# Memory stage of a macaron block: VectorE's second retrieve product in front of the residual store and the inverse deviation

## What is computed

```
x = x + 0.5 * ffn(layernorm(x))
x = x + attn(layernorm(x))
x = x + 0.5 * ffn(layernorm(x))

attn(x): keys   = (x @ Wk.T + bk) as 64 quaternions, each divided by its norm
         values = (x @ Wv.T + bv) as 64 quaternions
         memory = cumsum over positions of quat_mul(values, keys)
         r = quat_mul(memory, quat_conj(keys)) / sqrt(position)
         return x + (layernorm(r) * ln_g + ln_b) @ Wo.T + bo
ffn(x):  xr, xk = mixes of x and x of the position before
         return sigmoid(xr @ W_r) * (square(relu(xk @ W_k)) @ W_v)
```

## Time and profile before

| | |
|---|---|
| median of 3 runs | 636.75 us (635.14 to 639.82) |
| the profiled execution | 636.66 us |
| its span | 634.9 us |
| mean granted TensorE clock | 0.997 |
| first feed-forward, memory stage, second feed-forward | about 0 to 184, 184 to 460, 460 to 635 us |

### The profile page before, as it was taken

One profiled execution on the slowest core, in us unless ns is written; L12 is line 12 of the kernel. 1 busy time (PEld: TensorE's weight loads), 2 busy tenths in 40 slices (PEclk: granted clock), 3 DMA queues, 4 the chain that ended last, 5 costly groups with the idle time before them and its releaser, 6 DMA issues.

```text
span 634.9 us, 12143 instructions
## 1 busy us (share of the span) xinstructions
PE 607.8 (96%) x3284; PEld 513.9 (81%) x3285; DVE 561.6 (88%) x1160; ACT 466.9 (74%) x858; POOL 530.6 (84%) x616
## 2 busy tenths in 40 slices
PE   6999999999987999999999999998889899999997
PEld 4888898989866787778778777877668789898896
DVE  6999999998878999999999999999988778787773
ACT  5767677776567888888888888887467767777662
POOL 1788989887748999999999999998938898888863
PEclk9999999999998999999999999999999999999999
DMA  8740000000000000000000000000001111010111
GB/s 236 246 149 2 0 0 0 0 0 1 2 1 1 0 3 0 0 0 0 0 0 0 0 0 0 0 0 1 0 2 35 34 66 66 33 66 33 67 67 66
DMA packets 19272, 18.65 MB, mean 29 GB/s; under 512 B 1328, under 2 KB 19248, under 8 KB 19248
## 3 DMA queue, kind: packets, MB, share of 16 engines
q1 hardware_dynamic: 19248, 18.36, 9.1%
HBM read 9.97 MB, written 8.39 MB: 29 GB/s over the span
## 4 chain that ended last, share of the span: by engine, by line
PE 46%; POOL 27%; issue 19%; ACT 4%; DVE 3%; POOLq 1%; ACTq 0%; DVEq 0%
PE bank L1295 24%; PE bank L1343 16%; POOL rhalf L289 7%; POOL ret L296 6%; POOL kact L278 5%; POOL bhalf L271 4%; PE bank L1316 4%; POOL bhalf L269 1%; ACT xn L825 1%; POOL xr_lo L1152 1%; POOL rhalf L287 1%; PE bank L1286 1%; PE bank L1479 1%; PE bank L1362 1%; POOL xk_lo L303 0%
## 5 line engine op out<-in xcount | busy, mean ns | idle before, releaser
L1343 PE MATMUL bank<-wffn,kact 128*128 128x256 f32 x512 | 117.0, 382 | 3.3 <-DVE kact L427 3.3
L1423 PE MATMUL bank<-wkv,m_xnT 128*128 128x256 f32 x480 | 117.9, 389 | 2.1 <-ACT m_xnT L953 2.1
L1423 PEld LDWEIGHTS bank<-wkv,m_xnT 128*128 128x128 f32 x480 | 89.9, 192 | 24.2 <-ACT m_xnT L953 8.5
L1343 PEld LDWEIGHTS bank<-wffn,kact 128*128 128x128 f32 x512 | 95.0, 190 | 16.0 <-DVE kact L427 3.7
L303 POOL TENSOR_TENSOR xk_lo<-xk,xk_hi 128x1024 fp32r<-128x1024 f32 x30 | 71.0, 2368 | 40.4 <-ACT xk_hi L841 40.3
L1159 POOL TENSOR_TENSOR res<-res,gating_buffers 128x1024 f32 (+1 forms) x31 | 74.6, 2406 | 12.8 <-DVE gating_buffers L434 12.5
L645 DVE TENSOR_TENSOR xn<-bank,khat 128x1024 f32<-128x1024 f32 x64 | 77.7, 1216 | 2.1
L645 DVE TENSOR_TENSOR gating_buffers<-bank,khat 128x1024 f32<-128x1024 f32 x64 | 77.4, 1211 | 0.0
L1152 POOL TENSOR_TENSOR xr_lo<-xr,xr_hi 128x1024 fp32r<-128x1024 f32 x30 | 71.1, 2370 | 1.5
L1479 PE MATMUL bank<-wo_centred,normedT 128*128 128x256 f32 x256 | 66.3, 388 | 4.9 <-DVE res L682 2.1
L1295 PE MATMUL bank<-wffn_hi,xr_hi 128*128 128x256 f32 x240 | 67.4, 281 | 0.0
(11 more groups left out here) (143 smaller groups left out, 1597.6 us busy)
## 6 DMA issues: line engine op xcount, KB each, us to landing
res<-x SPq DMA_DIRECT2D x15, 512.0 KB, 4.2
out<-res SPq DMA_DIRECT2D x15, 512.0 KB, 2.9
res<-x SPq DMA_DIRECT2D x2, 256.0 KB, 2.9
out<-res SPq DMA_DIRECT2D x2, 256.0 KB, 2.1
wffn<-w_k SPq DMA_DIRECT2D x1, 256.0 KB, 5.0
wffn<-w_r SPq DMA_DIRECT2D x1, 256.0 KB, 5.7
wo<-w_o SPq DMA_DIRECT2D x1, 256.0 KB, 6.0
wffn<-w_v SPq DMA_DIRECT2D x1, 256.0 KB, 6.3
```

The costliest lines, as they stand in the source:

```text
L1343: last = nc.tensor.matmul(dst[:, i, :], x[:, f, i * P:(i + 1) * P], wffn[:, w, f, :], start=f == 0, stop=f == FC - 1)
L1423: last = nc.tensor.matmul(dst[:, i, :], m_xnT[:, f, i * P:(i + 1) * P], wkv[:, f, col:col + D], start=False, stop=f == FC - 1, skip_group_ ...
```

## The change

In VectorE's list of the memory stage, retrieve(j, b, 1) moves up by two places: it is issued right behind key_sum, ahead of the store of s - 3 and of ln_inverse of s - 1. All else, waits and semaphores too, is as before. The last step's own branch is untouched.

```diff
--- before.py
+++ after.py
@@ -718,11 +718,11 @@
                             next_stats(0)
                         if has(b, 2):
                             key_sum(j + 1, b)
+                        retrieve(j, b, 1)
                         if has(b, -3):
                             store_x(*at(j, b, -3))
                         if behind:
                             ln_inverse(*at(j, b, -1))
-                        retrieve(j, b, 1)
                         if has(b, 2):
                             key_inverse(j + 1, b)
```

## The result

The changed kernel takes 662.02 us in the median (661.12 to 662.96, 4 runs) against 637.47 before: ratio 1.038, 95% interval 1.036 to 1.040. Forecast were 660.2 us and a range of 656 to 665. The profiled execution has a span of 660.1 us against 634.9, 25.2 more.

A forecast was written before the change was run, and what follows sets the result against it. VectorE was taken to set the memory stage's pace, with the loop through the store just below; 22.6 us for 26 transitions plus 0.9 on the way out gave 23.5 on 636.66, so 660.2 us, range 656 to 665.

The forecast's parts named there:

- The store already is on time by a hair, and the loop through it is the second bound: Memory stage: PE's output waits for VectorE's store L682; that loop lies just below VectorE's own work, slack 0.25 us.
- The two numbers behind it: Loop from store through PE, ScalarE and VectorE back to store: 8.29 us without the product, 9.41 with it.
- What is late next is VectorE, retrieve 0 waits some 0.8 us: VectorE's first product of a memory-stage step would wait some 0.8 us for PE's sum_upto.
- retrieve 1 earlier, cost and gain nothing: VectorE's second product starts 0.67 us earlier for GpSimd's rhalf, which comes to it in its turn; gain 0.
- L615 costs nothing: VectorE's reciprocal, 1.12 us later, feeds ScalarE's ret_normalize, which has 0.8 us idle behind it; cost 0, other end 0.3.
- 22.6 us for 26 transitions: Memory stage, stores of s = 3 to s = 29: 26 steps, each going from 8.54 to 9.41 us.
- The way out, 0.9: At s = 30 PE's output and the store behind it come later; 0.9 us, bounds 0 and 1.0.
- Rival C, the clock falls: PE idling before each output lowers its clock, each step's keys take 3.54 us; 43 us more, 703 us; chance 0.04.
- the step with the added statistics: Near the memory stage's end (s = 28), statistics precede the store; led by VectorE's branch, +0.86 us, like the other steps.
- Rival A: Memory stage: VectorE's occupancy is the bound and PE absorbs the push; no change, 636.7 us; chance 0.07.
- B: PE's slack before the output counts in full, 0.31 us a step, 8 in all; 645 us; chance 0.05.
- D: VectorE's second product held the step; earlier, it removes a GpSimd-related wait, 6 us faster, 630.7 us; chance 0.03.

The follow-up runs named there:

- e1_store_first: Changed kernel with the store put back ahead of retrieve 1, leaving only the move past the inverse deviation; 637.52 us, ratio 0.9995 to the kernel before.
- e2_store_late: Changed kernel with VectorE's order key_sum, ln_inverse, retrieve 1, store; 666.69 us, ratio 1.046 to the kernel before.
- e6_store_last: Changed kernel with the store behind key_inverse, last in VectorE's step; 686.03 us, ratio 1.076 to the kernel before.
- e3_store_early: Changed kernel with the store right behind khat, ahead of the first bind product; 634.15 us, ratio 0.994 to the kernel before.
- e7_early_product_late: Kernel before with only the store moved, to right behind khat; retrieve 1 stays behind ln_inverse; 637.67 us, ratio 1.000 to the kernel before.
- e8_pe_order_before: Kernel before with PE's sum_upto 0 of the next step and sum_after 1 ahead of the output; 662.88 us, ratio 1.039.
- e4_pe_order: Changed kernel with PE's sum_upto 0 of the next step and sum_after 1 ahead of the output; 653.40 us, ratio 1.025 to the kernel before.
- e9_store_early_again: e3_store_early run once more, unchanged; 633.83 us, ratio 0.993 to the kernel before.
- e10_inverse_in_gap: e3_store_early with ln_inverse moved behind key_inverse, ahead of khat; 631.18 us, ratio 0.990 to the kernel before.

## Why the prediction was right, point by point

- *The store already is on time by a hair, and the loop through it is the second bound*: shown. e1_store_first leaves the store where it was and loses nothing; the changed order, e2_store_late and e6_store_last delay it by different amounts and have steps of 9.41, 9.53 and 10.28. The sum gave 9.41, 9.48 and 10.34.
- *The two numbers behind it*, 8.29 and 9.41: the changed kernel's steps are 9.412. The three stretches of the loop were met within 0.05: store to output 0.15, output to key_sum 6.86 (6.89 worked out), key_sum to the store's end 2.42 (2.37). The last is 0.05 longer because key_sum, now started from a wait, takes 0.60 to the next start and not 0.57.
- *What is late next is VectorE, retrieve 0 waits some 0.8 us*: 0.76.
- *retrieve 1 earlier, cost and gain nothing*: true of the changed kernel, and only there. With the store gone from that place it is worth 0.18 us a step (e3_store_early against e7_early_product_late), by the rows as a cover for the root, which the prediction did not see.
- *L615 costs nothing*: e1_store_first.
- *22.6 us for 26 transitions*: 20.77 + 0.77 + 2.63 = 24.17, of which 1.68 is the clock; without it 22.5.
- *The way out, 0.9*: measured 1.12 - 0.74 = 0.4. PE's output waited 0.91 us and the store behind it 1.18, as forecast; but ahead of the store of s = 30 a short VectorE instruction (L512) took 0.16 us where it had taken 1.09 (last section).
- *Rival C, the clock falls*: it was priced for every step, and it came once, where the wait was 2.68 us, for 1.68 us. The prediction took the step with the added statistics for one like the others, +0.86 us, and did not ask what its wait, 1.76 us before and a product longer now, would do to the clock. This is the largest term that was missing. The Trainium skill, page "TensorE: Matmul & The Clock Gate", section "Part 1: The HAM clock gate", has activity release the throttle and idling bring it back; the lower clock behind the wait of 2.68 us agrees with that. The page does not say that waits of about 1 us in each step are enough to make rival C the outcome; the prediction read that into it, and 24 waits of 1.17 us with no fall speak against it.
- *Rival A*, that VectorE's occupancy decides, which the prediction drew from the Trainium skill's page "Perfetto Trace Analysis", section "Identifying the Most-Contended Engine": the measurement is against it. VectorE's busy time went from 561.6 to 563.1 us while the time rose by 4%. *B* and *D* gave 645 and 630.7 and fall with the steps of 9.41.

- *The range, 656 to 665, "the forecast's own bounds"*: the sum of those bounds is 657 to 665, so its lower end is off by 1 us. Nothing hangs on it here.

The span grew by 25.2 us and not by 23.5, and the 1.7 between them are three misses: 1.6 more in the 26 transitions (the clock), 0.5 less on the way out, and 0.65 by which the stage's first store is later than the product explains. That the number came so close owes a little to their partly cancelling.

The 0.65 us lie before anything that the change touches. Of them 0.50 are there at the first products of the stage (VectorE's L596 stands at 184.53 us before and at 185.03 after), and the rest at its first key_sum (195.65 and 196.31). The two profiled executions differ from the start: over 8 to 16 us the granted clock was 1.00 in the one of before and 0.79 in the changed kernel's.

## What to carry to other kernels

An engine whose rows touch each other can be reordered at no cost only if no loop through another engine comes within the length of the moved instruction of its own step: add the loop up, from the consumer that frees the buffer round to itself, and compare it with the engine's own sum. A store that frees a single buffer belongs as early as its input allows, and best into the gap behind an instruction whose result the next one reads (here worth 0.6%). When a row shows a wait with no named releaser on an engine that looks full, see whether some store ended 0.1 us before it.

## What the runs showed of the hardware

**The granted clock behind a wait.** Inside a fall the granted clock is 0.50 (462 to 464 us in the changed kernel), otherwise 1.00. The falls looked at here came behind waits of PE. Waits of 2.68 (changed kernel), 2.75 (e2_store_late) and 3.56 us (e6_store_last) were each followed by outputs at half speed, 1.91 us for a set that takes 1.03. Shorter waits went both ways. Those of 1.17 us in the changed kernel, 1.76 in the kernel before and 2.04 in e6_store_last left the clock at full speed each time. One of 1.73 us near the end of the stage in e2_store_late did not, nor did one of 1.54 us early in e8_pe_order_before, where the same place in e4_pe_order, with 1.53 us, stayed at full speed. PE in these three, in this order:

```profile
484.37 1.11 PE L1479 MATMUL bank<-wo_centred,normedT 128*128 128x256 f32 x4 [1.73 <-DVE res L682]
...
485.49 1.91 PE L1479 MATMUL bank<-wo_centred,normedT 128*128 128x256 f32 x4
```

```profile
209.55 3.04 PE L1423 MATMUL bank<-wkv,m_xnT 128*128 128x256 f32 x8 [1.54 <-ACT m_xnT L953]
```

```profile
211.13 1.99 PE L1423 MATMUL bank<-wkv,m_xnT 128*128 128x256 f32 x8 [1.53 <-ACT m_xnT L953]
```

What decides in a short wait, no run here shows. At the stage's start, too, the clock falls in some executions and not in others, without regard to the change: over 184 to 196 us it was 0.86 before the change and after it, and 1.00 in e1_store_first, e3_store_early and e9_store_early_again. The eight key projections there take 3.5 to 3.7 or 2.0 us, so this is some 1.5 us of the spread between executions. Of the kernel before, sixteen further executions took 635.68 us at the highest mean clock, 0.999, and 639.14 at the lowest, 0.990. The changed kernel, one stretch (its bounds and length, busy us of PE, PEld, DVE, ACT, POOL, clock, then two columns on DMA):

```profile
184.00:196.00 12.00, 9.28 (x38) 6.99 (x37) 8.59 (x19) 7.12 (x14) 8.41 (x13) 0.86 0.00 0
```

and e9_store_early_again:

```profile
184.00:196.00 12.00, 8.81 (x42) 6.86 (x43) 9.97 (x21) 8.61 (x16) 8.40 (x13) 1.00 0.00 0
```

**A short VectorE instruction that ends when a GpSimd one does.** L512 works on 4 columns and takes 0.16 us with GpSimd idle. Beside GpSimd's additions it took 1.09 in the kernel before, and its end falls on the end of an addition, 449.60 and 449.58. The kernel before, timeline of both engines:

```profile
448.51 1.09 DVE L512 SCALAR_TENSOR_TENSOR shift<-mv,rstd 128x4 f32<-128x4 f32 x1
...
448.87 0.71 POOL L289 TENSOR_TENSOR rhalf<-gating_buffers 128x256 f32<-128x256 f32 x1
```

It is the same in all ten kernels in which L512 took longer than 0.16 us (its end lies 0.01 to 0.02 us behind an addition's), as in e3_store_early (445.52 and 445.50), e4_pe_order (464.86 and 464.84) and e10_inverse_in_gap (443.94 and 443.91), and for L596 in the kernel before (207.33 and 207.31). That the two engines hinder each other there is read from these coincidences; no run was made to test it.
